# Routing, scatters and the shared network moved into the tokens' pipeline of a two-layer transformer

## What is computed

```python
# layer 0
h = layernorm(x) * (1 + ca) + sa
x = x + ga * attention(h, qkv, wo)          # 16 heads of 16, rotary, causal; a score of exactly 0 counts as masked
h = layernorm(x) * (1 + cb) + sb
x = x + gb * sigmoid(xr @ W_r.T) * (square(relu(xk @ W_k.T)) @ W_v.T)   # xr, xk mix a token with the one before
# layer 1
h = layernorm(x) * (1 + ca) + sa
x = x + ga * layernorm(h + delta_scan(h @ Wq, h @ Wk, h @ Wv, beta) @ Wo + b_o)
h = layernorm(x) * (1 + cb) + sb
probs = softmax(h @ router_w + router_b)     # 16 experts, the best two of each token
# every expert takes its first 640 tokens, in the order of the tokens: silu(h @ wg) * (h @ wu) @ wd, inner width 352
x = x + gb * (h + shared_mlp(h) + weighted sum of the two experts' rows)
```

## Time and profile before

| what | us |
|---|---|
| median of 3 runs (2251.21 to 2266.96) | 2265.68 |
| the profiled execution's own time | 2265.7 |
| its span in the profile | 2264.0 |
| stage project / attend / tokens | 0 to 146 / 146 to 1369 / 1378 to 1710 |
| routing, shared network and scatters / experts | 1710 to 1901 / 1901 to 2264 |
| mean granted TensorE clock | 0.961 of full speed |

### The profile page before, as it was taken

The page is one execution under the profiler, slowest core; times in us unless marked ns, Lnnn a source line. Parts: engine busy times, 40 slices in busy tenths (PEclk is TensorE's granted clock), DMA queues, the critical chain, the costliest instruction groups (busy, mean ns, idle before and its releaser), DMA issues. The chain is left out here.

```text
span 2264.0 us, 29939 instructions
## 1 busy us (share of the span) xinstructions
PE 1963.9 (87%) x10325; PEld 826.0 (36%) x10325; DVE 1645.7 (73%) x2200; ACT 1408.6 (62%) x1894; POOL 926.7 (41%) x817
## 2 busy tenths in 40 slices
PE   7979999989999989998999995889858659999997
PEld 4432222222222222222222223556533226776775
DVE  6769999999999999999999993576556123333332
ACT  5748999989999889998899992556532001111110
POOL 5843434333334333443333431467542720433424
PEclk9979999999999999999999997999988779999999
DMA  5642211021111121143300002110001312444441
GB/s 204 207 135 43 43 31 22 10 64 24 31 22 31 45 43 31 22 127 116 91 24 13 3 3 78 38 37 1 1 1 47 110 45 92 101 101 93 115 99 24
DMA packets 124923, 133.93 MB, mean 59 GB/s; under 512 B 35161, under 2 KB 118962, under 8 KB 124080
## 3 DMA queue, kind: packets, MB, share of 16 engines
q1 hardware_dynamic: 110192, 118.09, 19.1%
q0 software_dynamic: 14592, 14.08, 3.6%
HBM read 97.08 MB, written 50.63 MB: 65 GB/s over the span
## 5 line engine op out<-in xcount | busy, mean ns | idle before, releaser
L1013 DVE SCALAR_TENSOR_TENSOR arena<-ps_s,arena 128x1024 f32<-128x1024 f32 (+1 forms) x1071 | 1147.6, 1140 | 55.8 <-ACT arena L979 45.7
L979 ACT ACTIVATE arena<-ps_s 128x1024 f32<-128x1024 f32 (+1 forms) x1194 | 1043.0, 930 | 129.8 <-PE ps_s L927 115.8
L927 PE MATMUL ps_s<-arena 128*128 128x512 bf16 (+3 forms) x2304 | 607.8, 367 | 76.2 <-DVE arena L1013 45.0
L943 PE MATMUL ps_o<-arena,values 128*32 128x512 f32 (+3 forms) x4608 | 566.3, 569 | 30.3 <-ACT arena L970 28.9
L1022 POOL TENSOR_SCALAR arena<-arena 128x512 f32<-128x512 f32 x123 | 236.3, 1921 | 533.8 <-ACT arena L984 533.7
L927 PEld LDWEIGHTS ps_s<-arena 128*128 128x128 bf16 x2304 | 155.3, 98 | 683.8 <-DVE arena L1013 505.7
L2135 POOL DMA_INDIRECT out<-values,slot_ids x80 | 123.8, 1548 | 304.7 <-DVE values L2099 276.4
L1950 ACT ACTIVATE arena<-g_ps_g 128x320 f32<-128x320 f32 (+1 forms) x96 | 42.1, 438 | 310.7 <-PE g_ps_u L1884 310.7
L943 PEld LDWEIGHTS ps_o<-arena,values 128*32 128x32 f32 x4608 | 94.2, 108 | 262.2 <-issue 180.4
L2072 DVE TENSOR_TENSOR arena<-g_ps_u,arena 128x320 f32<-128x320 f32 (+1 forms) x96 | 47.2, 492 | 168.2 <-ACT arena L1950 168.2
L1036 POOL TENSOR_SCALAR_AFFINE_SELECT arena<-arena 128x512 f32<-128x512 f32 (+3 forms) x146 | 81.1, 581 | 212.5 <-DVE arena L1013 212.5
(11 more groups left out here) (207 smaller groups left out, 1848.7 us busy)
## 6 DMA issues: line engine op xcount, KB each, us to landing
arena<-parts_dram SPq DMA_DIRECT2D x320, 64.0 KB, 2.3
parts_dram<-arena SPq DMA_DIRECT2D x32, 384.0 KB, 3.0
arena<-parts_dram SPq DMA_DIRECT2D x24, 512.0 KB, 7.0
slots_in_dram<-in_empty_slots SPq DMA_DIRECT2D x10, 1040.0 KB, 24.9
arena<-slots_in_dram SPq DMA_DIRECT2D x16, 650.0 KB
arena<-in_L_ffn_w_gate SPq DMA_DIRECT2D x16, 352.0 KB
arena<-in_L_ffn_w_up SPq DMA_DIRECT2D x16, 352.0 KB
arena<-in_L_attn_x SPq DMA_DIRECT2D x8, 512.0 KB, 4.2
```

The source lines that it names most:

```text
L927: last = pe.matmul(ps_s[:, unit.bank + i, p.at:p.at + p.width], m.k_stack[:, group.g % 2 * HG + p.head, p.kt * P:p.kt * P + P], q_stack[:, ...
L943: last = pe.matmul(ps_o[32 * p.head:32 * p.head + 32, p.w0:p.w0 + p.width], m.values_flat[:, at:at + 32], probs[:, job.at % PROB_BANKS, p. ...
L979: act.activation(probs[:, unit.slot:unit.slot + n], ps_s[:, unit.bank:unit.bank + n], ACT.Exp, scale=1.0 / DH ** 0.5).then_inc(exped, 1)
L1013: dve.scalar_tensor_tensor(p, ps_s[:, unit.bank:unit.bank + n], 0.0, p, ALU.not_equal, ALU.mult).then_inc(bank, 1)
```

## The change

1. **The token pipeline takes over routing, scatters and the shared network.** `phase_moe` is gone; its experts follow at the end of `phase_tokens`' programs, without an end of a stage between them. The pipeline has skews 0 to 7, so 15 steps. Skew 5: logits, softmax, the two best experts, places, and 8 scatters for the 4 tiles of that block; skew 6: `up` and `hide`; skew 7: `down` and `add_shared`. Counts of the blocks before are carried in `taken_so_far`. Routing now works on 4 tiles (128x64) instead of 32 (128x512).
2. **Silu is written as a Sigmoid** on ScalarE and one more product on VectorE; `up` uses the two halves of `ps_turn`, `down`, logits and counts use `ps_out`, in turns with the old users.
3. **Loads across the ends of stages.** The first two blocks of Q are loaded by `phase_project` (in its step 8), and the last two pieces of K by `phase_attend` (before: Q in `phase_attend`, and one piece of K). The attention rows and the x rows of the first two token blocks are loaded at the end of `phase_attend` instead of at the start of `phase_tokens`.
4. **Ends of stages.** The semaphores of a stage are cleared at the start of the next one (`retire`), and the barrier behind the clearing is gone.
5. **Attention's order.** At the opening of a block the first groups are weighed up to 4 places later (`OPENING` = 4), and the turning comes 4 places later.

```diff
-TURN_LAG = WEIGH_LAG + 6
+OPENING = 4
+TURN_LAG = WEIGH_LAG + OPENING + 6
...
-            while u < len(working) - 1 and working[u].jobs[-1].at < group.jobs[-1].at + WEIGH_LAG:
+            since_first = group.kt if group.kt < TT * group.j else TT * group.j
+            behind = WEIGH_LAG + (max(OPENING - since_first, 0) if group.block else 0)
+            while u < len(working) - 1 and working[u].jobs[-1].at < group.jobs[-1].at + behind:
...
             with sp.If(bounded(sp) > 0):
-                for w in range(2):
-                    sp.wait_ge(m.stored[w], 16 * 2)
-                load_q(0)
                 wait_parts_stored(m, sp)
-                load_first_k(m, sp, NB - 1, m.kload_last)
+                for b in range(NB - 2, NB):
+                    load_first_k(m, sp, b, m.kload_last)
...
+                for b in range(2):
+                    sp.wait_ge(o_stored[b], 64 * ((BLOCKS - NB) // 2 + 1))
+                    load_attn(m, sp, b)
                 store(BLOCKS - 2)
+                for b in range(2):
+                    last_tile = ((b + 1) * TT * D - 1) // (NH * (DH + 1))
+                    sp.wait_ge(probs_free, plan.weighed_through(BLOCKS - 1, last_tile))
+                    load_x_again(m, sp, b)
                 store(BLOCKS - 1)
...
-    nc.clear_and_free_semaphores(own)
-    nc.all_engine_barrier()
+    m.retired = own
...
+def retire(nc, m):
+    nc.clear_and_free_semaphores(m.retired)
+    m.retired = []
...
-    turns = Uses(mixed=3, attn=0, final=4, attended=1)
-    outs = Uses(attend=1, gate=2, value=2, delta=3)
+    turns = Uses(mixed=3, up0=6, up1=6, attn=0, final=4, up2=6, attended=1)
+    outs = Uses(down=7, attend=1, gate=2, value=2, logits=5, count=5, delta=3)
...
+            def open_up(b, i):
+                width = FM[i][1]
+                act.wait_ge(turned, turns.through(f"up{i}", b))
+                act.activation(silu[0:width], ps_turn[0:width, 0], ACT.Sigmoid).then_inc(opened, 1)
+
+            def exponentials(b):
+                act.wait_ge(maxed, b + 1)
+                act.activation(expd, shifted, ACT.Exp).then_inc(exped, 1)
...
+            def hide(b, i):
+                n = nm * b + i
+                width = FM[i][1]
+                dve.wait_ge(opened, n + 1)
+                then(dve.tensor_tensor(silu[0:width], ps_turn[0:width, 0], silu[0:width], ALU.mult))
+                if i == 0 and b:
+                    dve.wait_ge(out_made[1], outs.through("down", b - 1))
+                dve.tensor_tensor(hidden[0:width, i], ps_turn[0:width, 1], silu[0:width], ALU.mult).then_inc(turn_taken, 1)
...
-            staged([(2, mix), (4, residual), (2, mix_again), (1, add_attended), (4, add_delta), (2, combine),
-                    (3, lambda b: scan(b, 0)), (3, lambda b: scan(b, 1))])
+            staged([(2, mix), (4, residual), (2, mix_again), (7, add_shared), (1, add_attended), (4, add_delta), (2, constants),
+                    (6, lambda b: hide(b, 0)), (2, combine), (3, lambda b: scan(b, 0)), (6, lambda b: hide(b, 1)), (5, take_logits),
+                    (3, lambda b: scan(b, 1)), (5, choose), (6, lambda b: hide(b, 2)), (5, find_places)])
...
+            def scatter(b):
+                if b == 0:
+                    pool.wait_ge(m.zeroed, m.zeroed_expected)
+                pool.wait_ge(marked, 3 * b + 3)
+                pool.wait_ge(erow, b + 1)
+                for k in range(2):
+                    pool.wait_ge(placed, 2 * b + k + 1)
+                    for t in range(b * TT, b * TT + TT):
+                        pool.indirect_dma_start(
+                            out=m.slots_in[:, :], out_offset=bass.IndirectOffsetOnAxis(ap=m.scatter_at[:, k, t:t + 1], axis=0),
+                            in_=m.h_wide[:, t], in_offset=None, bounds_check=E_ * CAP - 1, oob_is_err=False).then_inc(scattered, 16)
...
-        for phase in (phase_project, phase_attend, phase_attend_unbounded, phase_tokens, phase_moe):
+        for phase in (phase_project, phase_attend, phase_attend_unbounded, phase_tokens):
```

More of the change, by code:

```diff
@@ L793, in scored_through, with weighed_through @@
         return max(job.unit.scored for group in self.groups if group.block == block for job in group.jobs) + 1
+    def weighed_through(self, block, kt):
+        return max(group.n for group in self.groups if group.block == block and group.kt <= kt) + 1
     def masked_through(self, group):
@@ new lines, in make_logits @@
+            def make_logits(b):
+                pe.wait_ge(turn_taken, turns.through("final", b))
+                for c in range(2):
+                    pe.wait_ge(out_taken[c], outs.before("logits", b))
+                    for t in range(2):
+                        at = b * BT + (2 * c + t) * P
+                        for k in range(KC):
+                            last = pe.matmul(ps_out[:, c, t * E_:t * E_ + E_], m.h_even[:, k, at:at + P], m.router[:, k, 0:E_],
+                                             start=k == 0, stop=k == KC - 1)
+                    last.then_inc(out_made[c], 1)
@@ L1463, in _ @@
+            pe.wait_ge(turn_taken, turns.through("up2", NB - 1))
+            pe.wait_ge(bank_taken, banks.through("spread1", NB - 1))
+            pe.wait_ge(k_copied, 2 * NB)
+            turn_rows(0, 0)
+            for c in range(2):
+                pe.wait_ge(out_taken[c], outs.through("down", NB - 1))
+            experts(pe, step)
         @block.scalar
```

841 lines of the change are left out of this document (390 added, 451 removed).

## The result

The changed kernel takes 2248.4 us (median of 11 runs, 2242.8 to 2252.7), the kernel before beside it 2267.0 (11 runs, 2251.2 to 2269.9): a ratio of 0.992, 95% interval 0.990 to 0.994. So 0.8% faster, not 2.2%: 33 us above the forecast, and just above the upper end of the range. The profiled execution has a span of 2241.0 us and took 2242.8, the fastest of the eleven: against it the forecast missed by 28 us, and the other 5.6 are the way from it to the median.

A forecast was written before the change was run, and what follows sets the result against it. The loss was placed from 1369 to 1901 us, in the token pipeline's ramp, drain and scatters. 2264 - 6 - 8 - 6.5 - 1 - 30 + 1 = 2213.5 us span, plus 1.7: 2215 against 2265.7, range 2172 to 2248.

The forecast's parts named there:

- Project to attend (-6): Start of attend: Q and K loaded earlier, first scores at about 147.5 and no second load stall; net -6 us.
- openings (-8): Block openings in attend: weighing the first groups later cuts VectorE's idle time by 8 us (bounds 0 and -20).
- Attend to tokens (-7.5): Between attend and tokens: loads already there, -6.5 us, and one barrier less, -1 us.
- The pipeline, 517 to 487 (-30): First token turn to first expert: a step-by-step walk through the engines, plus 5 us for hops and clock; -30 us.
- t=0 to 4 as before (3, 16, 25, 24, 33.5): The pipeline's first five steps keep their old lengths, in us, counted between the ends of turn_attended.
- t=5: 38.5, t=6: 50, t=7: 52.5, t=8: 50: Middle pipeline steps, in us, as routing, up and down join; t=7 is the only step with all skews.
- t=8 to 11: 47, 44, 41 ... t=14: Late pipeline steps: 50, 47, 44, 41 us for t=8 to 11, then 30, 22.5 and 5 us.
- The scatter gap vanishes: End of the token stage: only 8 scatters remain behind the last routing, beside up and down; within the -30 us.
- Table loads: ScalarE's function table changes for Exp in eight steps: hidden in waits, priced at nothing; 21 us if not covered.
- the scatters stop all engines again: Rival: each burst of 8 scatters in the token pipeline halts the engines, 90 us in all; 2305 us, chance 0.08.
- TensorE bounds the full steps: Rival: scatters are covered and TensorE bounds full pipeline steps, 455 us instead of 487; 2175 us, chance 0.2.
- The pipeline couples too much: Rival: one shared ring of engines and banks makes every step from 5 on 5 us longer; 2260 us, chance 0.17.

The follow-up runs named there:

- e1: Changed kernel with TensorE's attend_out ahead of down, turn_mixed and mix_keys again, and VectorE's add_attended ahead of add_shared; 2244.9 us, ratio 0.989 to the kernel before.
- e8: On e3: TensorE's turn_mixed, attend_out and mix_keys ahead of down, turn_attn earlier, ScalarE's take_attn ahead of exponentials; 2232.6 us where the kernel before took 2211.0.
- e2: Changed kernel with a block's 8 scatters moved behind gain of the next step; 2248.2 us, ratio 0.991 to the kernel before.
- e9: Changed kernel in which up sums over only half of the features, so the result differs; 2228.9 us on the chip where the kernel before took 2211.0.
- e7_again: Repeat of e7: e4_again's kernel with a wait between groups of 8 scatters; 2207.8 us, ratio 0.973. The first run took 2204.6 us, on another chip.
- e4_again: Repeat run: changed project and attend stages, with the old token pipeline, routing, scatters and shared network of the kernel before; 2247.5 us, ratio 0.991.
- e3: Changed kernel with the edits of both e1 and e2; 2241.0 us, ratio 0.988 to the kernel before.

## Why the prediction was wrong, step by step

1. **Project to attend (-6) and openings (-8): right.** First scores at 147.03 (forecast 147.5), no second stall: 7.1 us of the two (4.9 and 2.2), forecast 6. VectorE's last operation of attend moved from 1368.2 to 1354.1, 14.1 for 14, so the openings brought 7 for 8.
2. **Attend to tokens (-7.5): right.** The first turn came 20.9 us earlier, where the three terms sum to 21.5.
3. **The pipeline, 517 to 487 (-30): this failed.** It took 512.8, -4 (519.0 in the second execution). The work was priced rightly: TensorE 46.8 us in the full step for 46.5, VectorE 40.0 for 40, POOL 29.7 for 32, ScalarE 24.2 for 21. The walk through the steps was not, and its steps as they stand sum to 482.0, not 482.5:
   - *"t=0 to 4 as before (3, 16, 25, 24, 33.5)"*: 119.5 instead of 101.5. 4.3 us are a slip: counted between ends of `turn_attended`, the walk left out `modulate` and `difference` when it changed to counting from `mix` (the rows of before sum to 105.8). The other 13.7 were a term put at nothing: the new stages were taken to leave the ramp's steps as they were. 8 of them are TensorE's new order (e1), which I had printed and read only for the full step; t=4 came back to 33.6 only in e8, which changes ScalarE's order too. e1 also shows that putting the ramp right gives only 0.7 us of the stretch back.
   - *"t=5: 38.5, t=6: 50, t=7: 52.5, t=8: 50"*: 38.4, 49.9, 54.2, 52.4. The sizes were nearly right for a partly wrong reason. `add_delta` was at 19.6 us after `mix` (forecast 18.3), but TensorE's 46.8 us of work (forecast 46.5) and 7.3 of waits are longer by a little (e2: no gain without the scatters; e9: 4.6 less with 5.2 us less of TensorE's work). I had written that no engine reaches the end alone. TensorE does, once its waits at the turn of the step, which the walk did not add to it, are counted.
   - *"t=8 to 11: 47, 44, 41 ... t=14"*: the drain took 9 us more, 6.3 of them in t=11, where TensorE waited 11.3 us for `hide` behind `add_delta` and then ran `up` at 6.74 instead of 3.60 us (the clock is 0.75 in this step). The 5 us for hops and clock covered less than half of the 13 that the drain and the full steps wanted.
4. **"The scatter gap vanishes": true, and worth 42 us** (e7_again against e4_again). The rebuilt stretch gave all but 4 of them back, or all. The comparison that the prediction missed is old pipeline without the standstill: 476.8 us. In the old order the shared network is a TensorE-bound run of 15.5 us a block with the scatters beside it; in the new one it stretches the steps from 33.6 to 50 and more and lengthens the drain by three steps.
5. **Table loads: right for the full steps** (the load at 1609.63 ends at 1610.9, and VectorE reads the exponential at 1612.88; the next copy for TensorE begins at 1611.10, when its products have just ended). In t=11 one is on the path: load at 1804.35, and VectorE waits 1.33 us for the exponential. **Bursts of 8: right**, 11.5 us for 10.3. **Experts +1: nearly**, +2.1 (364.8 for 362.7).

The rivals: "the scatters stop all engines again" did not come. "TensorE bounds the full steps" had the right engine and the wrong price, since it left out the waits at a step's turn. "The pipeline couples too much", each step longer, gave 2260; and the measured 2248 lies nearer to it than to the forecast. The number is in part luck: the rival had 5 us more in each step from 5 on and nothing in the ramp, but the ramp made 18 of the 31 us and the ten steps behind it 13. Its mechanism is borne out in kind: e1, e2 and e3 moved waits of single stages, and got 1, -2 and 3 us of the stretch, no more than two executions of one kernel differ by.

## What to carry to other kernels

Before merging a stage into a pipeline, ask what its loss is made of: here 42 of 517 us were one standstill, which a wait every eighth scatter removes, and the kernel with that wait and the earlier loads (2207.8 us beside 2246.9 for the change and 2267.4 before) beats everything that the rebuilding gave. On the chip without the standstill the same wait made the kernel before 0.5% slower, so where it stands is to be measured. A full step of a ring of engines is worked out for each engine as its work plus its waits for its own buffers; when two such chains are within some us of each other, removing the wait on one buys nothing. A ramp is walked with the new order of every engine, not taken over from the old one. And before a difference of some us between two profiles is read, one kernel is profiled twice.

## What was not expected of the hardware

- 64 scatters sent in a row hold up the other engines by up to 52 us, until 6 to 7 us behind the last one; with rows of at most 32 and pauses the longest wait beside them is 10.7 us, and TensorE works for 43 of 43 us beside the second of two.
- The same kernel took 2211 us on one chip and 2251 to 2270 on the others, while e7 took 2204.6 there and 2207.8 elsewhere. On the first the rebuilt e8 is slower than the kernel before (1.010, 1.009 to 1.012). The changed kernel itself was not run there.
- Less work and less waiting did not give TensorE their whole gain: in t=7 of e8 and e9 the granted clock was 0.97 and 0.96 instead of 1.00, and the products at the turn of the step took 1.5 and 1.7 us more. The changed kernel itself had 0.91 there in its second execution.
- A 128x4 cast of VectorE takes 0.17 us, but 1.90 where POOL's `difference` runs beside it. The next `mix` starts 0.5 us behind the end of `difference` for it:

```profile
1569.21 1.89 POOL L2086 TENSOR_TENSOR arena<-arena 128x1024 f32<-128x1024 f32 x1 [11.18 <-ACT arena L1744]
1569.24 1.90 DVE L1985 CAST scatter_at<-arena 128x4 uint32<-128x4 f32 x1
...
1571.55 0.17 DVE L1985 CAST scatter_at<-arena 128x4 uint32<-128x4 f32 x1
```

The Trainium skill ("SBUF — State Buffer", Who interferes with whom) names casts of VectorE among the operations that can be locked out for the whole of a GpSimd instruction; the trace agrees, for an operand of only 4 elements a partition.
